# Second MLP of a two-layer sequence kernel: down-projections by seven block products instead of eight

## The reference

```python
attn_out = softmax((x @ Wq) @ (x @ Wk).T * scale) @ (x @ Wv) @ Wp + bp
cms_out  = gelu(attn_out @ cW1 + cb1) @ cW2 + cb2 + one_hot(target_codes)
modifier = gelu(concat([attn_out, cms_out]) @ mW1 + mb1) @ mW2 + mb2
x1 = clip(x + cms_out + modifier, 0, 1)
h  = gelu(x1 @ W_down[role] + b_down[role])
y  = x1 + h @ W_up[role] + b_up[role]
out = layernorm(y) * gamma[role] + beta[role]
```

## Time and profile before

| | us |
|---|---|
| median of 3 runs | 2095.6 |
| lowest, highest | 2093.02, 2096.95 |
| the profiled execution | 2094.39 |
| its span, first to last instruction | 2092.6 |

### The profile page before, as it was taken

How to read it: one execution, slowest core, us unless ns; L and a number is a source line. 1 busy time by engine, 2 the same in 40 slices (tenths; PEclk the granted TensorE clock), 3 DMA queues, 4 the chain that set the end, 5 groups by cost and what they waited for, 6 DMA issues and landing times.

```text
span 2092.6 us, 26680 instructions
## 1 busy us (share of the span) xinstructions
PE 2077.7 (99%) x9644; PEld 1719.5 (82%) x9644; DVE 1313.0 (63%) x2089; ACT 922.0 (44%) x1604; POOL 274.2 (13%) x282
## 2 busy tenths in 40 slices
PE   8999999999999999999999999999999999999998
PEld 7888888888788888888888888888878888888886
DVE  6576675546767667455677667555476766754557
ACT  5464443333356444333335544443334645433342
POOL 0011112210101102112000110112100111121101
PEclk9999999999999999999999999999999999999999
DMA  7411211122321121221460112111342011112233
GB/s 283 162 31 41 71 66 51 61 71 97 141 81 41 51 86 36 71 70 47 164 205 31 51 51 76 61 48 66 110 145 92 21 51 55 62 61 71 71 106 91
DMA packets 42367, 169.70 MB, mean 81 GB/s; under 512 B 5624, under 2 KB 9720, under 8 KB 34808
## 3 DMA queue, kind: packets, MB, share of 16 engines
q1 hardware_dynamic: 42096, 167.97, 23.6%
q10 hardware_dynamic: 144, 0.03, 0.0%
HBM read 146.97 MB, written 21.01 MB: 80 GB/s over the span
## 4 chain that ended last, share of the span: by engine, by line
PE 95%; DVE 2%; ACT 1%; issue 1%; DMA 0%; SPq 0%; ACTq 0%; DVEq 0%
PE psum L579 86%; PE psum L871 2%; PE psum L834 2%; PE psum L654 1%; PE psum L676 1%; PE psum L874 1%; PE psum L847 1%; DVE acc L1447 0%; DVE fpart L1217 0%; PE psum L859 0%; PE psum L837 0%; ACT wup L1112 0%; PE psum L677 0%; PE psum L656 0%; DMA fraw<-fuse_in 0%
## 5 line engine op out<-in xcount | busy, mean ns | idle before, releaser
L579 PE MATMUL psum<-hs,wd 128*128 128x512 f32 x3072 | 717.9, 389 | 1.8 <-DVE acc L1447 1.8
L579 PEld LDWEIGHTS psum<-hs,wd 128*128 128x128 f32 x3072 | 576.0, 188 | 123.5 <-DVE acc L1447 3.5
L1447 DVE TENSOR_TENSOR acc<-psum,acc 128x512 f32<-128x512 f32 x448 | 294.5, 685 | 175.5 <-PE psum L579 174.3
L579 PE MATMUL psum<-cop,wsm 128*128 128x512 f32 x1416 | 354.7, 389 | 0.0
L579 PE MATMUL psum<-aop,wsm 128*128 128x512 f32 x1320 | 333.0, 389 | 0.0
L579 PE MATMUL psum<-aop,wsc 128*128 128x512 f32 x1320 | 311.3, 389 | 0.0
L579 PEld LDWEIGHTS psum<-cop,wsm 128*128 128x128 f32 x1416 | 265.8, 188 | 55.1
L579 PEld LDWEIGHTS psum<-aop,wsm 128*128 128x128 f32 x1320 | 247.8, 188 | 51.4
L579 PEld LDWEIGHTS psum<-aop,wsc 128*128 128x128 f32 x1320 | 247.5, 188 | 51.4
L1074 ACT ACTIVATE hs<-psum,bias 128x512 fp32r<-128x512 f32 x144 | 98.2, 682 | 394.5 <-PE psum L579 394.5
L1217 DVE TENSOR_TENSOR hs<-zt,hs 128x512 fp32r<-128x512 f32 x256 | 181.0, 707 | 125.6 <-ACT zt L1075 125.6
(11 more groups left out here) (167 smaller groups left out, 2214.6 us busy)
## 6 DMA issues: line engine op xcount, KB each, us to landing
w1m<-m_in SPq DMA_DIRECT2D x32, 1024.0 KB, 4.9
w1c<-c_in SPq DMA_DIRECT2D x32, 512.0 KB, 3.5
w<-c_in SPq DMA_DIRECT2D x32, 512.0 KB, 3.5
w<-m_in SPq DMA_DIRECT2D x32, 512.0 KB, 3.5
gains<-roles_in SPq DMA_DIRECT2D x30, 512.0 KB, 4.7
fw<-fused SPq DMA_DIRECT2D x6, 2048.0 KB, 10.0
fused<-fw SPq DMA_DIRECT2D x4, 2048.0 KB, 7.5
xmid<-x SPq DMA_DIRECT2D x4, 2048.0 KB, 6.4
```

What stands on the lines that cost most here:

```text
L579: mm = nc.tensor.matmul(out, lhs(a), rhs(b), start=(start and n == 0), stop=(stop and n == total - 1), skip_group_check=reopened)
L1447: nc.vector.tensor_tensor(dst, d_out[o][:, :], dst, ALU.add).then_inc(acc_done, 1)
```

## The change

In the second MLP, the down-projections of units 9 to 14 (`FAST`, six a pass, 24 in all) are done by seven block products too, called D1 to D7 below. The blocks are two halves of the 512 output features, the two hidden blocks of the unit, and the two token blocks. A block product is 2 x 3 = 6 matmuls, so a unit has 42.

- GpSimd makes four sums of down-weight blocks of 128x256 for each such unit (`combine_down`), queued behind `combine` of the same unit.
- The down weights are split in seven parts of 128x256 (`split_part` and `low_part`) where there was one step of 128x1024, and stand in five slots. The up weights of the second MLP turn over four slots, which makes room.
- Four sums of hidden quarters are made (`hidden_sum`, VectorE) and split (`split_sum`, ScalarE; `low_sum`, VectorE). H10 is no longer needed in parts of its own. Full-precision Gelus go to where the low parts come to lie, which makes room in `zt`.
- D5 and D3 gather in one pair of PSUM banks, D1 and D2 as well, D6, D7 and D4 in another pair, on top of a ScalarE copy of D1 (`copy_down`). VectorE adds six results of 128x1024 (`fast_add`) where it added eight of 128x512.
- TensorE's order in a turn is P1 P5 D5 P6 D3 P2 D1 P7 D6 P4 D7 D2 P3 D4; in turn 15 each of D5, D3, D1, D6 and D7 stands one up product earlier. Turn 9 has the plain down of unit 8.
- In turns 10 to 15 z12 and the H01 steps of unit u-1 stand at the head of unit u's queues on VectorE and ScalarE, ahead of `copy_p1(u)`; they stood at the end of unit u-1's, and `copy_p1` ahead of them.
- The order of the last unit's adds and adapter steps is changed, and unused branches for `BY_POOL` are gone.

```diff
+FAST = range(NG + 1, UNITS - 1)
+DOWN = (P5, P3, P1, P6, P7, P2, P4)
+UP = (P1, P5, P6, P2, P7, P4, P3)
+SPLIT = (P5, P7, P6, P4)
+W1_SLOTS, W2_SLOTS = 4, 5
...
+            def combine_down(p, u):
+                f = fasts(p, u)
+                pool.wait_ge(w2_loaded, 16 * (UNITS * p + u + 1))
...
+                nc.gpsimd.tensor_tensor(comb2[:, 0, :], w2_block(2, 1), w2_block(2, 2), ALU.add).then_inc(w2_sums, 1)
+                pool.wait_ge(w2_sums, 4 * f + 1)
+                nc.gpsimd.tensor_tensor(comb2[:, 1, :], comb2[:, 0, :], w2_block(1, 1), ALU.subtract).then_inc(w2_sums, 1)
+                nc.gpsimd.tensor_tensor(w2_block(2, 1), w2_block(1, 1), w2_block(2, 1), ALU.subtract).then_inc(w2_sums, 1)
+                pool.wait_ge(d_lo, d_at(p, u) + 1)
+                pool.wait_ge(w2_sums, 4 * f + 2)
+                nc.gpsimd.tensor_tensor(comb2[:, 0, :], w2_block(1, 2), comb2[:, 1, :], ALU.subtract).then_inc(w2_sums, 1)
...
+            def fast_down(p, u, *which):
+                n, f, a0 = UNITS * p + u, fasts(p, u), acc_at(p, u)
+                for i in which:
+                    pe.wait_ge(d_lo, d_at(p, u) + DOWN.index(i) + 1)
+                    if i in SPLIT:
+                        pe.wait_ge(ht_lo, 4 * f + SPLIT.index(i) + 1)
+                    else:
+                        pe.wait_ge(h_lo[{P1: H11, P2: H01, P3: H00}[i]], n + 1)
+                    if i in (P6, P2):
+                        pe.wait_ge(d_copied, f + 1)
+                    else:
+                        pe.wait_ge(acc_done, {P5: a0 - (1 if fast(u - 1) else 2), P3: a0 + 1, P1: a0 + 2, P7: a0 + 3, P4: a0 + 4}[i])
...
+            # ScalarE
+            def second_unit(p, layer, u):
+                then = fast(u - 1)
+                if then:
+                    weight_part(p, u, P2)
+                    hidden(p, layer, u - 1, H01)
+                    copy_p1(p, u)
+                    split_sum(p, u - 1, P4)
+                    weight_part(p, u, P7)
+                    split_part(p, u - 1, P2)
+                copy_p5(p, u)
+                weight_part(p, u, P4)
+                if then:
+                    split_part(p, u - 1, P4)
+                copy_u2(p, u)
+                weight_part(p, u, P3)
+                if then:
+                    copy_down(p, u - 1)
+                hidden(p, layer, u, H00)
+                if fast(u):
+                    split_part(p, u, P5, P3)
+                    weight_part(p, u + 1, P1)
+                    hidden(p, layer, u, H11)
+                    weight_part(p, u + 1, P5)
+                    split_part(p, u, P1, P6)
+                    hidden(p, layer, u, H10)
+                    weight_part(p, u + 1, P6)
+                    split_sum(p, u, P5)
+                    split_part(p, u, P7)
+                    split_sum(p, u, P7, P6)
...
+            # VectorE
+            def second_unit(p, layer, u):
+                then = fast(u - 1)
+                if then:
+                    make_z12(p, u - 1)
+                    weight_part(p, u, P2)
+                    hidden(p, u - 1, H00)
+                    low_sum(p, u - 1, P7)
+                    hidden_sum(p, u - 1, P4)
+                    fast_add(p, u - 1, P5)
+                    low_sum(p, u - 1, P6)
+                    weight_part(p, u, P7)
+                    hidden(p, u - 1, H01)
+                    low_part(p, u - 1, P2)
+                    low_sum(p, u - 1, P4)
+                    fast_add(p, u - 1, P3)
+                weight_part(p, u, P4)
+                if then:
+                    low_part(p, u - 1, P4)
+                weight_part(p, u, P3)
...
+                    make_z22(p, u)
+                    if then:
+                        fast_add(p, u - 1, P6)
+                        low_part(p, u, P5, P3)
+                    weight_part(p, u + 1, P1)
+                    if then:
+                        fast_add(p, u - 1, P7)
+                        fast_add(p, u - 1, P2)
+                    else:
+                        add(p, layer, u - 1, 1, *range(KC))
+                    weight_part(p, u + 1, P5)
+                    low_part(p, u, P1, P6)
+                    hidden_sum(p, u, P5)
+                    hidden_sum(p, u, P6)
+                    hidden_sum(p, u, P7)
+                    weight_part(p, u + 1, P6)
+                    low_sum(p, u, P5)
+                    hidden(p, u, H11)
+                    if then:
+                        fast_add(p, u - 1, P4)
+                    add_x(p, layer, u)
+                    low_part(p, u, P7)
```

More of the change, by code:

```diff
@@ L334, in h_source, with h_raw, h_operand, h_sum @@
             return {H00: bank_a(), H11: zt[:, 2, :], H10: bank_b(), H01: zt[:, 1, :]}[h]
-        def h_raw(h):
-            return zt[:, {H00: 3, H11: 2, H10: 0, H01: 1}[h], :]
+        def h_raw(u, h):
+            m, b = h_place(h)
+            if fast(u) and h == H10:
+                return t34_raw[:, 0, LO, :]
+            return hs_raw[:, b, LO, m, :]
+        def h_operand(i, part):
+            return {P1: hs[:, 1, part, 1, :], P2: hs[:, 1, part, 0, :], P3: hs[:, 0, part, 0, :], P5: hs[:, 0, part, 1, :],
+                    P6: t2[:, (0, 3)[part], :], P7: t34[:, 0, part, :], P4: t34[:, 1, part, :]}[i]
+        def h_sum(i):
+            return {P5: hs_raw[:, 0, LO, 1, :], P6: zt[:, 3, :], P7: t34_raw[:, 0, LO, :], P4: t34_raw[:, 1, LO, :]}[i]
         block = ctx.enter_context(nc.Block())
@@ L780, in down @@
                         (lambda a, m=m: wd[:, a, m, o * P:(o + 1) * P], lambda c, m=m: hs[:, b, c, m, :],
-                         (h_lo[heres[m]], n + 1) if o == 0 else None) for m in range(MC)]).then_inc(dn_done, 1)
+                         (h_lo[heres[m]], (plain_downs(p, u) if heres[m] == H10 else n) + 1) if o == 0 else None)
+                        for m in range(MC)]).then_inc(dn_done, 1)
+            def fast_down(p, u, *which):
[10 more added lines that the diff above has]
+                        pe.wait_ge(acc_done, {P5: a0 - (1 if fast(u - 1) else 2), P3: a0 + 1, P1: a0 + 2, P7: a0 + 3, P4: a0 + 4}[i])
+                    out = d_b if i in (P6, P7, P4) else d_a
+                    first = i in (P5, P1)
+                    for o in range(2):
+                        mm = product(out[:, o, :], [(lambda a: part(u, i)[:, a, o * P:(o + 1) * P], lambda c: h_operand(i, c), None)],
+                                     first, True, not first)
+                    mm.then_inc(dn_done, 1)
             def mlps(p):
@@ new lines, in mlps @@
+                    hidden(p, u, H11)
+                    down_part(p, u)
+                    weight_part(p, u + 1, P4 if u + 1 == NG else P7)
+                    make_z12(p, u)
+                    hidden(p, u, H10)
+                    hidden(p, u, H01)
+            def second_unit(p, layer, u):
[17 more added lines that the diff above has]
+                weight_part(p, u, P3)
+                if not then:
+                    add(p, layer, u - 1, 0, *range(KC))
+                if fast(u):
+                    if not then:
+                        low_part(p, u, P5, P3)
+                    make_z22(p, u)
+                    if then:
+                        fast_add(p, u - 1, P6)
+                        low_part(p, u, P5, P3)
+                    weight_part(p, u + 1, P1)
+                    if then:
+                        fast_add(p, u - 1, P7)
+                        fast_add(p, u - 1, P2)
+                    else:
+                        add(p, layer, u - 1, 1, *range(KC))
[6 more added lines that the diff above has]
+                    low_sum(p, u, P5)
+                    hidden(p, u, H11)
+                    if then:
+                        fast_add(p, u - 1, P4)
+                    add_x(p, layer, u)
+                    low_part(p, u, P7)
+                else:
+                    fast_add(p, u - 1, P6)
+                    hidden(p, u, H00)
+                    adapter_part(p, 0)
+                    make_z22(p, u)
+                    fast_add(p, u - 1, P7)
+                    fast_add(p, u - 1, P2)
+                    adapter_part(p, 1)
+                    hidden(p, u, H11)
+                    down_part(p, u)
+                    hidden(p, u, H10)
+                    fast_add(p, u - 1, P4)
+                    up_part(p, 0)
+                    make_z12(p, u)
```

326 lines of the change are left out of this document (220 added, 106 removed).

## The result

The changed kernel takes 2154.85 us (median of 4 runs, 2152.55 to 2156.74), the kernel before 2095.01 (4 runs): ratio 1.0285, 95% interval 1.0267 to 1.0303. I had forecast 2125, within 2067 to 2141. The sign was right, and the time fell outside the range: 60 us were lost where I had 30.

What follows compares the result with a forecast made beforehand. TensorE, busy 99% of the span, was taken as the bound. Per pass 16.36 us lost against 8.63 won gave +7.73, over four passes +30.9 on 2094.39: 2125.3 us, range 2067 to 2141.

Steps and rivals of the forecast that it cites:

- Removed work: TensorE, turns 10 to 15: 42 down matmuls for 48, 1.36 us less a turn, 32.6 us in four passes.
- VectorE's load: VectorE, steady turns 11 to 14: 21.8 us of steps in a 28.56 us turn; busy time near 25 us.
- The order and the disturbance: VectorE's queue up to z12, held by GpSimd: P6' 2.71 us late in turns 11 to 14; turn 15 loses 5.52.
- level behind it: Turns 11 to 14, before D3: add P5 ends at 23.14 us, just when D3 is due.
- the step that failed: TensorE: granted clock 1.00 in both profiled stretches, matmuls 0.2267 us each; no term for slower matmuls.
- E: VectorE, z22 to z12: 18 steps each keep the engine 0.68 us, not 0.60; 2153 us, chance 0.08.
- B: Second MLP: w1 lands late or GpSimd falls behind, so only the third combination collides; 2097.5 us, chance 0.17.
- C: Second MLP: GpSimd and VectorE don't meet on the path; turns 11 to 14 lose 0.22 us; 2071, chance 0.23.
- A: Second MLP: three GpSimd collisions with VectorE on the path; 2125 us, own range 2108 to 2140, chance 0.45.

Runs made afterwards that it cites:

- b2: Changed kernel with VectorE's and ScalarE's queues reordered by need, turn 15's down products placed as elsewhere, adapter steps and a weight step moved later: 2074.96 us, ratio 0.9905.
- e2: Changed kernel with GpSimd's combinations of the second MLP cut to 8 columns, all waits kept, products of other weights: 2085.05 us, ratio 0.9951.
- e3: Changed kernel with z12 moved ahead of add P4, the x add and low part P7 in VectorE's queue: 2152.52 us, ratio 1.0277.
- e1: Changed kernel with extra matmuls, results unread, filling TensorE's waits before P6, D5 and D3: 2136.2 us, ratio 1.0196.
- e5: Kernel before, with ScalarE's copy of P1 held back by 4, 6, 7 and 9 extra copies in passes 0 to 3: 2146.12 us, one run.

## Why the prediction was right in sign and wrong in size

**Removed work.** 1.36 us a turn, 32.6 in all: right. b2 shows that it can be had: 20 us of it arrived.

**VectorE's load.** Forecast near 25 us a turn by recorded durations and 200 us more in all; measured 26.48 us in turn 12 of pass 2, and 1565.1 - 1313.0 = 252. Each waiting behind GpSimd is counted as busy. The added 128x1024 adds take 1.22 us, within 0.01 of the like of the earlier trace rows, and 1.14 from start to start where I had 1.13.

**The order and the disturbance.** Low P3 was forecast to end at 5.49 and ended at 5.54, weight P1 at 7.26 and 7.25, z12 at 18.47 and 18.55; P6' was forecast 2.71 us late and shows 2.70 to 2.71 in most turns. From start to start of its matmuls that costs 2.87 (3.22 in turn 12, where the recorded wait is 3.05), a little more than the recorded wait. Turn 10 was spared, as forecast. Turn 15: forecast 1.66 and 5.52 in all, measured 1.58 and 1.58 + 3.96 = 5.54. e2 shows that the taking of turns with GpSimd was the cause that I said, and e3 that the add of D5 was level behind it, as I said.

**The clock: the step that failed.** The sum ran "4 x 2.71 + 5.52 = 16.36 lost" with every matmul behind a wait at the spacing of the earlier trace rows. I had read the granted clock, 1.00 in both stretches, and used it only to say that the rates were at full speed. That number is of a TensorE that never idles; it could not be carried over to a kernel that I had just given a 2.7 us pause in every turn. Measured in pass 2, the turns 11 to 15 take 33.13, 31.91, 33.11, 31.61 and 36.66 us against 28.56, 23.6 us more in all: 17.4 in waits and 6.3 in the matmuls behind them (1.70, 0.13, 1.69, 0.18 and 2.56; the two small ones are with the clock at 1.00, the three large ones with it at its lower level for a while). Over the four passes, counted the same way, the waits come to 68.3 us where I had 65.4, and the matmuls behind them to 26.0 where I had nothing, some 3 of them the 0.1 that follows every wait: 2125.3 + 2.9 + 26.0 = 2154.2, where 2154.85 was measured. e1 and e5 show it from both sides: the same waits filled give the speed back, and waits put into the kernel before take it.

**The rivals.** E gave 2153, within 2 us, and was wrong in mechanism: with its 18 full durations the wait before P6 would have been 4.1 us, not 2.7, and e1's kernel, with the same VectorE queue, would not have gained. In the profile after, steps of 0.68 us still start 0.60 apart (1475.55, 1476.15, 1476.75, 1477.35), so E's reading of the Trainium skill, VectorE: DVE Perf Modes, "The DRAIN you can't avoid", isn't borne out. The same section adds that a next operation that isn't held starts earlier, and these rows agree with that; I had left it out. B and C were told apart from A by the wait alone, as I had written they would be. What the list lacked was a clock term on A, B and C alike; with it A is 2154.

**What stays open.** Why 9 of 16 nearly equal waits are followed by slow matmuls and 7 aren't. In passes 0 to 2 it goes from turn to turn in alternation, in pass 3 it doesn't. Length alone doesn't decide it: one of the seven is the longest, 3.05 us, and of the waits of 2.0 to 2.1 us 8 of 16 are followed by slow matmuls in e3, 1 of 4 in e2.

## What to carry to other kernels

Whoever forecasts a new wait on TensorE has to price it twice: its length, and the matmuls behind it at the lower clock. Here waits up to 1.7 us cost their length and 0.3 us; of those of 2.0 to 2.1 us some, and of those of 2.3 us and over most, cost some 1.2 to 3 us more. When an engine's queue gets denser, order it by when each result is needed, and follow every consumer round the whole turn, those level with the first late one and those queued behind a DMA too; moving one step only handed the wait to the next (e3), moving all of them turned 2.8% slower into 1% faster (b2).

## What the runs showed of the hardware that I had not expected

**The clock in short.** A single wait of 2.34 us on an otherwise full TensorE was followed by slow matmuls in three cases of four (six took 2.90 us where 1.62 is usual behind a wait); filling matmuls whose results nobody reads kept it at 0.998, at no cost, since they ran where TensorE would have stood.

**GpSimd and VectorE.** They took turns in all the places where the forecast had them meet; a VectorE step of 128x256 took 1.50 us (0.42 alone). The Trainium skill, SBUF — State Buffer, "SBUF: two separate sides", calls the port that they share an exclusive lock, held for a whole instruction. The rows agree: one side's step is held for the rest of the other's instruction, not slowed in proportion, and an engine that is busy 17% of the span took 2.3 us from each turn.
